# ScalarE lays the masks into the score banks, GpSimd adds the output bias and scatters the spline's deltas

## What is computed

```python
# layer 0 attention: 16 heads of 128, on the twice normalised x
q, k = rope(x @ wq.T + bq), rope(x @ wk.T + bk);  v = x @ wv.T + bv
attn = softmax(where(causal, -inf, q @ k.T / sqrt(128)))
x = x + (attn @ v) @ wo.T + bo + layernorm(x)
...
# layer 0 spline: each token adds four deltas to four neighbouring columns of x
out = zeros.at[token, tok_dims].set(delta);  x = x + out
# layer 1 attention: 16 heads of 16, a query sees a band of 64 keys behind it (two chunks of 64)
scores = where(band, q @ k.T * scale, finfo.min);  x = x + (softmax(scores) @ v) @ w_out.T
```

## Time and profile before

| | us |
|---|---|
| median of 3 runs (1037.38 to 1038.44) | 1038.16 |
| the profiled execution | 1038.18 |
| its span, first to last instruction | 1036.4 |
| TensorE busy | 987.3 (95%) |
| VectorE busy | 774.0 (75%) |
| ScalarE busy | 700.0 (68%) |
| GpSimd busy | 330.5 (32%) |

### The profile page before, as it was taken

One profiled execution on the slowest core, in us unless ns is written; L12 is line 12 of the kernel. 1 busy time (PEld: TensorE's weight loads), 2 busy tenths in 40 slices (PEclk: granted clock), 3 DMA queues, 4 the chain that ended last, 5 costly groups with the idle time before them and its releaser, 6 DMA issues. The chain is left out here.

```text
span 1036.4 us, 19376 instructions
## 1 busy us (share of the span) xinstructions
PE 987.3 (95%) x6919; PEld 817.8 (79%) x6948; DVE 774.0 (75%) x1525; ACT 700.0 (68%) x1959; POOL 330.5 (32%) x276
## 2 busy tenths in 40 slices
PE   8999999999999999999998987889899999999997
PEld 4888888888999889988998876767788789774444
DVE  5998867767676676766757889899998744567774
ACT  5888876677767776677763337687788635458882
POOL 2352333322333223332320120044555310107672
PEclk9999999999999999999999998999999999999999
DMA  6321000000000001000205000000000000028652
GB/s 204 103 61 62 2 1 1 2 1 1 2 1 1 1 1 36 1 2 1 82 5 144 1 1 1 1 2 2 1 2 2 2 1 2 6 67 267 225 174 82
DMA packets 31841, 40.23 MB, mean 39 GB/s; under 512 B 8192, under 2 KB 23296, under 8 KB 31744
## 3 DMA queue, kind: packets, MB, share of 16 engines
q1 hardware_dynamic: 31744, 38.98, 12.1%
HBM read 36.74 MB, written 2.23 MB: 38 GB/s over the span
## 5 line engine op out<-in xcount | busy, mean ns | idle before, releaser
L350 POOL TENSOR_TENSOR roped_q<-roped_q,sin_q 128x512 f32<-128x512 f32 x64 | 82.0, 1281 | 299.8 <-DVE sin_q L497 299.8
L1675 ACT ACTIVATE win_P<-banks,win_neg_max 128x128 f32<-128x128 f32 x256 | 91.1, 382 | 25.9 <-DVE win_neg_max L1752 25.5
L350 POOL TENSOR_TENSOR roped_k<-roped_k,sin_k 128x512 f32<-128x512 f32 x64 | 83.2, 1300 | 48.0 <-DVE sin_k L497 48.0
L404 ACT ACTIVATE P<-banks,neg_max 128x128 f32<-128x128 f32 x256 | 90.2, 372 | 10.5 <-DVE neg_max L522 10.4
L440 ACT ACTIVATE oT_hi<-banks,bv_col 128x512 fp32r<-128x512 f32 x64 | 44.0, 687 | 73.0 <-PE banks L670 73.0
L1610 POOL TENSOR_TENSOR win_P<-win_P,win_inv 128x512 f32<-128x512 f32 x64 | 66.8, 1044 | 75.0 <-DVE win_inv L1757 74.9
L413 ACT ACTIVATE sin_k<-banks 64x512 f32<-64x512 f32 x128 | 75.9, 593 | 11.1 <-PE banks L37 9.6
L525 DVE SCALAR_TENSOR_TENSOR oT_lo<-banks,bv_col,oT_hi 128x512 fp32r<-128x512 f32 x64 | 47.9, 748 | 43.1 <-ACT oT_hi L440 42.5
L413 ACT ACTIVATE sin_q<-banks 64x512 f32<-64x512 f32 x128 | 75.9, 593 | 3.7 <-PE banks L37 1.4
L632 PE MATMUL banks<-WO_lo,oT_hi 128*128 128x256 f32 x256 | 72.9, 285 | 0.0
L496 DVE SCALAR_TENSOR_TENSOR roped_k<-banks,qk_bias,cos 128x512 f32<-128x512 f32 x64 | 48.0, 750 | 31.8 <-ACT sin_k L413 31.8
(11 more groups left out here) (432 smaller groups left out, 3144.0 us busy)
## 6 DMA issues: line engine op xcount, KB each, us to landing
ret_V<-moe_gate_rows SPq DMA_DIRECT2D x16, 512.0 KB, 5.0
ctx<-moe_gate_rows SPq DMA_DIRECT2D x16, 512.0 KB, 5.0
X<-in_x SPq DMA_DIRECT2D x4, 512.0 KB, 6.9
stage<-in_wqT SPq DMA_DIRECT2D x4, 512.0 KB, 4.3
stage<-in_wvT SPq DMA_DIRECT2D x4, 512.0 KB, 6.2
stage<-in_woT SPq DMA_DIRECT2D x4, 512.0 KB, 4.9
ctx<-in_ctxT SPq DMA_DIRECT2D x4, 512.0 KB, 5.9
out<-X SPq DMA_DIRECT2D x8, 256.0 KB, 2.4
```

Of the source, the lines that this page charges most:

```text
L350: nc.gpsimd.tensor_tensor(roped[w][:, p, :], roped[w][:, p, :], sin_part[w][:], ALU.add).then_inc(roped_sum[w], 1)
L404: ins = nc.scalar.activation(P[:, i, :], SC[:, i * 128:(i + 1) * 128], ACT.Exp, bias=neg_max[:, r % 2, i:i + 1], accum_out=exp_sum[:, r % ...
L1675: ins = nc.scalar.activation(P[:, h % 2, s, i, :], SC[2 * (h % 2) + s][:, i * 128:(i + 1) * 128], ACT.Exp, bias=neg_max[:, h % 2, at:at + ...
```

## The change

**Causal mask.** For every head but the first, ScalarE copies the mask into the bank SC with one activation, `lay_mask(u)`: it waits for the exponentials of head u and stands in the order behind sin_q, or behind the exponentials themselves in the last steps, which have no projection. TensorE's scores of head u+1 wait for it and keep `start=False`. 63 of 64 mask matmuls go.

**Band masks.** For ticks 2 to 31 the second of a tick's two band matmuls goes, and `lay_band(h)` on ScalarE fills that bank, behind the first half of the exponentials of tick h+1. TensorE's scores of tick h+2 wait for it. The first bank keeps its matmul, which stands ahead of the wait.

**Output bias.** `add_const` moves from VectorE in step 3 of a group to GpSimd in steps 3 and 4, half a group in each, behind the sums of the products; the statistics wait for its own semaphore.

**Scatter.** Of the spline batches that the window stage finishes, 4 to 15 are scattered by GpSimd, with two buffers of their own: 4 to 7 at once after the first power, the others two ticks ahead of the tick in which VectorE takes their statistics. The statistics stay on VectorE and wait for GpSimd.

**xT_full.** Its evacuation moves on ScalarE from behind oT_hi to behind PT.

The diff, cut to its core:

```diff
 # phase_attn0, GpSimd
+                def add_const(g, i):
+                    pool.wait_ge(out_added, 2 * g + i + 1)
+                    nc.gpsimd.tensor_tensor(pair(g, i), pair(g, i), out_bias[:].rearrange("p (a n) -> p a n", a=1).broadcast_to([128, 2, D]), ALU.add).then_inc(const_added, 1)
...
                     step(t, t % 2)
+                    if t > HEADS0 and t % HEADS0 in (3, 4):
+                        add_const(t // HEADS0 - 1, t % HEADS0 - 3)
 # ScalarE
+                def lay_mask(u):
+                    if live(u, STEPS - 1):
+                        act.wait_ge(exps_done, u + 1)
+                        nc.scalar.activation(SC[:].rearrange("p (h n) -> p h n", h=GROUP), four(mask[:]), ACT.Copy).then_inc(mask_laid, 1)
...
                             ins.then_inc(rotated[w], 1)
+                            if w == 0:
+                                lay_mask(u)
...
+                    else:
+                        lay_mask(u)
                     if live(u, STEPS):
                         act.wait_ge(p_transposed, u + 1)
                         wait(act, pv_done, u)
                         nc.scalar.activation(flat(PT[:]), PO[:], ACT.Copy).then_inc(PT_ready, 1)
+                    if g + 1 < NG and r - 1 in prepared_at(g):
+                        i = prepared_at(g).index(r - 1)
+                        evacuate_xT((g + 1) * GROUP + i, i, g + 1)
...
-                    if g + 1 < NG and r - 1 in prepared_at(g):
-                        i = prepared_at(g).index(r - 1)
-                        evacuate_xT((g + 1) * GROUP + i, i, g + 1)
 # VectorE
-                def add_const(g):
-                    for i in range(2):
-                        dve.wait_ge(out_added, 4 * g + 1 + i)
-                        nc.vector.tensor_tensor(pair(g, i), pair(g, i), out_bias[:].rearrange("p (a n) -> p a n", a=1).broadcast_to([128, 2, D]), ALU.add).then_inc(out_added, 1)
...
-                    dve.wait_ge(out_added, 4 * g - 1 + i)
+                    dve.wait_ge(const_added, 2 * g - 1 + i)
...
-                    if r == 3 and 0 < g < NG:
-                        add_const(g - 1)
 # TensorE
-                        wait(pe, out_added, 4 * ug - 2)
+                        wait(pe, out_added, 2 * ug)
...
-                    wait(pe, exps_done, u)
+
                     if u == 0:
                         pe.wait_ge(consts_made, 2)
-                    nc.tensor.matmul(SC[:], ident_b[:], four(mask[:]), start=True, stop=True)
+                        nc.tensor.matmul(SC[:], ident_b[:], four(mask[:]), start=True, stop=True)
+                    else:
+                        pe.wait_ge(mask_laid, u)
 # phase_window
-        spread = sb("win_spread", [128, 2, D])
+        spread = sb("win_spread", [128, 4, D])
...
+        SHARED, AT_ONCE = 4, 4
 # GpSimd
+                def finish(b):
+                    at = 2 + b % 2
+                    wait(pool, pool_scattered, 2 * (b - SHARED) - 2)
+                    scatter(nc, nc.gpsimd, pool, pool_scattered, 2 * (b - SHARED) + 1, X, kept["sp_hot"], kept["sp_delta"], spread[:, at:at + 1, :], slice(b, b + 1)).then_inc(pool_scattered, 1)
...
                 power(PARTS[0]).then_inc(rstd_ready, 1)
+                for b in range(SHARED, SHARED + AT_ONCE):
+                    finish(b)
...
+                    if h + 2 < len(FINISHED) and (FINISHED[h + 2] or 0) >= SHARED + AT_ONCE:
+                        finish(FINISHED[h + 2])
 # ScalarE
+                def lay_band(h):
+                    act.wait_ge(exps_done, 2 * h + 2)
+                    nc.scalar.activation(SC[2 * (h % 2) + 1].rearrange("p (h n) -> p h n", n=128), band[:], ACT.Copy).then_inc(band_laid, 1)
...
                     if h < TICKS:
                         exps(h, 0)
+                    if 0 <= h - 1 < TICKS - 2:
+                        lay_band(h - 1)
 # VectorE, finish_batch: as before for b < 4, else
+                        dve.wait_ge(pool_scattered, 2 * (b - SHARED) + 2)
 # TensorE
-                    for s in range(2):
+
+                    for s in range(2 if h < 2 else 1):
                         nc.tensor.matmul(SC[2 * (h % 2) + s], ident_b[:], flat(band[:]), start=True, stop=True)
+                    wait(pe, band_laid, h - 1)
```

More of the change, by code:

```diff
@@ L277, in v_at @@
             return [((r + 2) // 4, (r + 2) % 4)] if r < 14 or g + 1 < NG else []
+        pair = lambda g, i: X[:, 4 * g + 2 * i:4 * g + 2 * i + 2, :]
         def run(eng, step):
@@ L1111, in ctx_columns, with scatter @@
     return view[:, :, b * S:(b + 1) * S] if isinstance(b, int) else view[:, :, bass.ds(b * S, S)]
-def scatter(nc, dve, done, count, X, hot, delta, spread, some):
+def scatter(nc, tensor, eng, done, count, X, hot, delta, spread, some):
     n = some.stop - some.start
     by_column = lambda ap: ap.rearrange("p b (t j) -> p b t j", j=4)
-    nc.vector.tensor_tensor(by_column(spread), hot[:, some, :].rearrange("p b (t a) -> p b t a", a=1).broadcast_to([128, n, 64, 4]),
+    tensor.tensor_tensor(by_column(spread), hot[:, some, :].rearrange("p b (t a) -> p b t a", a=1).broadcast_to([128, n, 64, 4]),
                             delta[:, some, :].rearrange("p b (a j) -> p b a j", a=1).broadcast_to([128, n, 64, 4]), ALU.mult).then_inc(done, 1)
-    dve.wait_ge(done, count)
-    return nc.vector.tensor_tensor(X[:, some, :], X[:, some, :], spread, ALU.add)
+    eng.wait_ge(done, count)
+    return tensor.tensor_tensor(X[:, some, :], X[:, some, :], spread, ALU.add)
 def phase_spline(nc, a, sem, sb_, bank, X, ident, mean, var_eps, rstd, minus_half, stats, ln_tmp, banks, w, kept, ahead_loaded, n_ahead):
@@ L1413, in _ @@
                 dve.wait_ge(residual_ready, B)
-                scatter(nc, dve, scattered, 1, X, hot, delta, wide[:, FIRST, :], FIRST).then_inc(scattered, 1)
+                scatter(nc, nc.vector, dve, scattered, 1, X, hot, delta, wide[:, FIRST, :], FIRST).then_inc(scattered, 1)
                 dve.wait_ge(scattered, 2)
```

11 lines of the change are left out of this document (8 added, 3 removed).

## The result

The changed kernel takes **1028.2 us** (median; 1027.4 to 1029.5), the kernel before 1038.1: a ratio of 0.9907 with a 95% interval of 0.9889 to 0.9924. The forecast was 1023.2, in a range of 1015.5 to 1031. So the direction and the range held, and of the 15.0 us forecast 9.9 came: two thirds. The profiled execution of the changed kernel took 1027.45 us (span 1025.7), 10.7 less than that of before.

| stretch | forecast | measured |
|---|---|---|
| first attention, to its last weighing | -8.3 | -5.6 |
| from there to the window's first maximum | 0 | -1.6 |
| window, first to fourth maximum | -1.0 | +0.2 |
| window, fourth to eighteenth (early ticks) | -6.2 | -3.4 (a tick 5.02 to 4.78) |
| window, eighteenth to last (late ticks) | +0.5 | -0.1 (4.44 to 4.43) |

What follows compares the result with a forecast made beforehand. TensorE was taken to bound the first attention, with VectorE close behind in the window and nearly without idle in its early ticks. From 1038.2 us, -8.3 (first attention) and -6.7 (window) gave 1023.2 us, range 1015.5 to 1031.

Steps and rivals of the forecast that it cites:

- The mask's slot and its fill: First attention: 63 mask matmuls of 0.21 us leave TensorE, 63 ScalarE activations of 0.60 us come; -8.3 us in all.
- the ring on ScalarE: First attention, steady step: oT_hi to PT packs to 5.72 us with the fill, PT may start after 6.04; 0.32 left.
- 0.25 us of slack meet 0.21: First attention: the weighing's slack behind PT's end, 0.25 us, covers the 0.21 us taken from TensorE; a step becomes 7.83.
- laps of 0.57 us more: First group, steps 1 to 6: exponentials wait for VectorE's maximum, so the fill adds 0.57 us in five laps, +2.9 us.
- The cover: Output bias off VectorE: worth nothing now, but keeps steps 18, 34 and 50 from losing about 0.6 us each.
- keeps those steps' rings short: First attention: xT_full's evacuation moves into the 1.40 us before oT_hi, nothing in a TensorE-bound step; cost 0.
- The ring of 4.27 us: Window tick: scores, maximum, four exponentials, band fill and release sum to 4.27 us; with additions late ticks 4.5, +0.5 us.
- the third rival: Window: GpSimd blocks VectorE, +0.4 us in 14 early ticks, window gives 5.6 less, 1028.8 us; chance 0.12.
- Not everything hid: Denies the rival that everything hides: first group's ring gives way, full 13.2 us, early ticks 4.4, 1015.3 us; chance 0.15.
- The band's ring: Window rival: release and queueing make it 4.8 us in all 28 ticks, window +0.9, 1030.8 us; chance 0.17.
- The fill is not long: Denies the rival that writing the mask into PSUM is long: at 1.3 us, about 1062 us, slower than before; chance 0.05.
- the scores do start earlier: Denies the rival that PT holds the weighing, so scores keep their time: first attention +3.5, 1035 us; chance 0.05.

## Why the forecast was right or wrong

**The mask's slot and its fill: right, the slack behind PT too large.** The fill's length, the vanished idle time before sin_k and the ring on ScalarE were as forecast, and with early transposes a step falls by the slot and a little more. The step that failed is "0.25 us of slack meet 0.21". It took the release distance from the weighing's matmul; the engine's first waiting instruction is its weight load, which began 0.20 us behind PT and can begin 0.04 behind. From the weighing of head 11 to that of head 59, 48 steps saved 7.7 us (0.16 each) where 48 x 0.21 = 10.1 were forecast. These 2.4 us are most of the 2.7 missing in the first attention; the terms below nearly cancel. The kernels with early transposes give them back in a plain step (7.81).

**Group 0: right, with a lap priced too high.** Forecast were laps of 0.57 us more; the one shown has 0.42. Counted on the weighings, the five laps cost 1.7 us (2.9 forecast), head 11 cost 0.7 (0.6). Heads 60 and 61, not in the forecast, are where the fill also costs: the steps behind head 59 lost 0.2 us in place of gaining 0.6. With the five steps behind the laps, which gained 0.6 us and not 1.05, this makes up most of what the laps saved.

**The bias and xT_full: right that they bring nothing alone, wrong on what they protect.** The bias on GpSimd takes 1.29 us an operation, and nobody waits for it:

```profile
L359 POOL TENSOR_TENSOR X<-X,out_bias x6: 1288/1293/1303, 176.3 to 436.9; 128x512 f32<-128x512 f32 x6
```

The cover was put at 0.6 us in each of three steps; it is 1.6 us. The step that failed took the 1.04 us of the earlier trace rows for the lateness after the change too, though the fill itself makes k later. The evacuation's place was put down as "keeps those steps' rings short" without a price; it is 3.7 us.

**The late ticks: right, with the ring binding one tick in four.** The ring of 4.27 us measured 4.29; with the other work of a tick the mean is 4.43 where 4.5 was forecast. (By the forecast's own numbers its additions are 0.38, 0.31 and 0.40, not 0.35, 0.31 and 0.3, and the mean 4.54.) The saved band matmul is eaten: 4.44 with it. The forecast had something else come on top of the ring in three ticks of four; those ticks stay as long as they are when the fill leaves the ring, so there it is the other work alone that sets them.

**The early ticks: the third rival, in part.** Forecast was 4.58 with the stretched normalising "in rows 11" at 1.19 us. The rival's mechanism is there, and stronger in a few ticks: 1.56 us, four ticks of fourteen, 0.19 us a tick. Without the meeting they take 4.59. The forecast gave the rival 1028.8 us by another size (0.4 in every tick). That this lies near the measured 1028.2 is luck: the first attention's 2.7 us make up what the rival lacks. The Trainium skill (SBUF — State Buffer, Who interferes with whom) says that a VectorE operation in a two-port mode, which a tensor_scalar can enter, and a GpSimd operation exclude each other for the whole instruction. The rows agree: the two VectorE instructions end at 694.55 and 695.36, each 0.15 us behind the GpSimd one beside it (694.40 and 695.21).

**The other rivals.** Not everything hid (steps of 7.89, group 0 longer). The band's ring is not 4.8 but 4.29. The fill is not long, and the scores do start earlier.

**The window's start: wrong.** -1.0 was forecast, +0.2 came. The scatter's part alone brought 1.9 us there (12.1 before, 10.2 with the band by matmul). The step that failed had the scores wait for the fill from tick 2 on only as a ring of steady length. In the ramp ScalarE is busy with exponentials without a break until the first fill, TensorE runs dry for 1.56 us, and the clock falls behind it. That costs 2.1 us, settled by the kernel with two more matmuls; 1.4 of them are the wait.

**Between the attentions: -1.6 us that nobody forecast.** Nothing of the change is there, and they are luck as far as the forecast goes. What differs is the clock: of before first, then of after, the same work.

```profile
547.00:549.00 2.00, 2.00 (x6) 1.43 (x5) 1.70 (x5) 0.02 (x1) 0.00 (x0) 0.50 0.12 21
615.00:618.00 3.00, 3.00 (x16) 3.00 (x15) 2.92 (x17) 0.00 (x0) 0.00 (x0) 0.51 0.00 0
```

```profile
540.00:544.00 4.00, 2.47 (x14) 1.89 (x15) 3.10 (x7) 2.44 (x4) 0.00 (x0) 1.00 0.25 42
609.00:612.00 3.00, 2.61 (x24) 2.37 (x24) 2.90 (x18) 1.04 (x2) 0.00 (x0) 1.00 0.00 0
```

The kernel before runs at half clock twice in this stretch where the changed one doesn't. The kernels of this study differ there by up to 1.7 us, with no edit near: from the last maximum of the attention to the first of the window it is 138.8 to 140.5 us (141.1 in the one with all transposes early, whose last steps are longer). Which of them fall to half clock at these two places was not explained, and each trace is one execution: the four of the changed kernel lie up to 2.1 us apart, with a mean clock of 0.992 in the shorter ones and 0.989 in the longer. So the 1.6 us are not shown to be the change's. It is also why a part undone in one kernel does not always give in the total what its own stretch shows.

## What to carry to other kernels

Read slack on the instruction that waits, not on the one that computes: on TensorE that is the weight load. Here 0.09 us of slack too many in the forecast took 0.05 us from every step, over a quarter of the 8.3 us forecast there. Work moved onto an engine with 0.3 us of room changes the price of everything else in that ring: two side edits that were worth 0.6 us alone protected 5 and 4 us once the fill was in. Where a moved operation makes a fast engine wait, look at the start of the stretch apart from its steady part, and at the granted clock behind the wait.

## What the runs showed of the hardware

- ScalarE writes a 128x512 bf16 constant from SBUF into PSUM in 0.583 us (63 times, 0.580 to 0.602) and in 0.612 in the window (30 times, up to 0.682): no dearer than reading PSUM.
- The weighing's weight load begins 0.04 us behind the end of the activation that it waits for.
- A normalising pair of VectorE (128x256, twice) takes 0.73 us alone and 1.56 beside two GpSimd operations of 0.61 and 0.73 us; each VectorE instruction ends 0.15 us behind the GpSimd one.
- Of nine traces in which TensorE waits 1.56 to 1.74 us at the window's start (0.57 us busy of 2 in the changed kernel), eight show a granted clock of 0.50 soon behind it, for 3.4 or 6.8 us, and one stays at 1.00. None of the five traces without the wait shows it. The wait costs 1.4 us to the fourth maximum, a half clock of 3.4 us another 0.7.
